# A two-layer graph network kernel: counting at 3.2 instead of 2.67 windows per lot, half of the one-hots on VectorE

## What is computed

```python
def reference(x, src, dst, edge_type_8, L0_gnn_weight, L0_gnn_bias, L1_gnn_W, L1_gnn_b):
    edge_index = jnp.stack([src, dst])
    h = jnp.maximum(_layernorm(x, axis=-1), 0.0)
    # layer 0: messages are h[src] @ weight[edge_type], summed at dst, plus bias
    x = x + _L0_gnn_ref(h, L0_gnn_weight, L0_gnn_bias, edge_index, edge_type_8)
    h = jnp.maximum(_layernorm(x, axis=-1), 0.0)
    # layer 1: dinv[dst] * dinv[src] * (h @ W)[src] summed at dst over the edges and a
    # loop at each node, plus b, then leaky_relu with slope 0.2
    x = x + _L1_gnn_ref(h, edge_index, L1_gnn_W, L1_gnn_b)
    return x
```

## Time and profile before

| | |
|---|---|
| median of three runs | 2302.07 us |
| lowest and highest | 2300.12 and 2308.04 us |
| the profiled execution's own time | 2306.06 us |
| its span in the profile | 2304.3 us |
| busy share of the span: PE, ACT, POOL, DVE | 87%, 70%, 71%, 53% |
| mean granted clock of PE | 0.953 |

### The profile page before, as it was taken

One profiled execution on the slowest core, in us unless ns is written; L12 is line 12 of the kernel. 1 busy time (PEld: TensorE's weight loads), 2 busy tenths in 40 slices (PEclk: granted clock), 3 DMA queues, 4 the chain that ended last, 5 costly groups with the idle time before them and its releaser, 6 DMA issues.

```text
span 2304.3 us, 44662 instructions
## 1 busy us (share of the span) xinstructions
PE 2007.3 (87%) x14354; PEld 1797.4 (78%) x14354; DVE 1219.7 (53%) x3510; ACT 1608.9 (70%) x3919; POOL 1643.0 (71%) x1740
## 2 busy tenths in 40 slices
PE   1567788887888898879899899999999999999897
PEld 1456777776787887768788889898888898989676
DVE  7446567667568666766656633323223232334267
ACT  4646677786878888678777877776767777676440
POOL 5577777777777777777766777777777777777414
PEclk9698999999999999999989999999999999999999
DMA  9446567656766776667776777765766666666485
GB/s 289 121 123 189 177 200 225 210 186 201 244 218 222 252 232 203 187 218 241 233 246 197 238 256 243 228 194 170 222 200 190 191 196 191 183 190 162 105 225 168
DMA packets 353088, 470.37 MB, mean 204 GB/s; under 512 B 113158, under 2 KB 264886, under 8 KB 352726
## 3 DMA queue, kind: packets, MB, share of 16 engines
q0 software_dynamic: 79072, 216.18, 31.9%
q1 hardware_dynamic: 228246, 165.07, 24.5%
q10 hardware_dynamic: 45536, 86.22, 10.2%
HBM read 348.61 MB, written 118.71 MB: 203 GB/s over the span
## 4 chain that ended last, share of the span: by engine, by line
PE 60%; POOL 13%; issue 7%; ACT 7%; DMA 5%; DVE 4%; ACTq 1%; DVEq 0%; POOLq 0%; SPq 0%
PE ps_slot L1599 21%; PE ps_slot L1659 13%; PE ps_proj L1615 13%; POOL rows_f L1099 12%; PE ps_aux L1659 9%; DMA rows_f<-table,idxT 3%; PE ps_slot L1629 3%; ACT gap_f L1338 2%; ACT staging_f L1275 2%; ACT wide_f L1331 1%; DMA abuf_f<-counts_d 1%; DVE hots_f L1495 1%; DVE hots_f L1492 1%; ACT onehot_f L1346 1%; ACT acc_f L1261 1%
## 5 line engine op out<-in xcount | busy, mean ns | idle before, releaser
L1099 POOL DMA_INDIRECT rows_f<-table,idxT x1617 | 1538.2, 951 | 510.3 <-issue 473.8
L1599 PE MATMUL ps_slot<-onehot_f,rows_f 128*128 128x128 f32 x6468 | 870.4, 287 | 150.7 <-DMA rows_f<-table,idxT 121.8
L1599 PEld LDWEIGHTS ps_slot<-onehot_f,rows_f 128*128 128x128 f32 x6468 | 824.8, 200 | 184.3 <-DMA rows_f<-table,idxT 134.7
L1338 ACT ACTIVATE gap_f<-iota,keyT 128x128 bf16<-128x128 bf16 x1617 | 528.6, 394 | 81.1 <-ACT staging_f L1275 49.6
L1275 ACT ACTIVATE staging_f<-ps_slot 128x400 bf16<-128x400 f32 x800 | 345.8, 500 | 182.2 <-PE ps_slot L1629 179.2
L1492 DVE TENSOR_TENSOR hots_f<-ps_slot,keys_f 128x400 bf16<-128x400 bf16 x800 | 285.2, 357 | 303.5 <-PE ps_slot L1629 299.5
L1615 PE MATMUL ps_proj<-w0t,acc_f 128*128 128x256 f32 x1600 | 375.8, 389 | 0.0
L1659 PE MATMUL ps_slot<-wide_f,stash_f 128*128 128x512 f32 (+1 forms) x1410 | 345.2, 390 | 1.6 <-ACT wide_f L1331 1.5
L1346 ACT ACTIVATE onehot_f<-gap_f 128x384 f32<-128x384 bf16 x539 | 277.5, 515 | 96.6 <-PE ps_slot L1599 96.4
L1416 DVE TENSOR_TENSOR acc_f<-ps_slot,acc_f 128x256 f32 x539 | 227.2, 422 | 219.5 <-PE ps_slot L1599 151.3
L1615 PEld LDWEIGHTS ps_proj<-w0t,acc_f 128*128 128x128 f32 x1600 | 303.2, 195 | 45.4 <-issue 1.6
(11 more groups left out here) (156 smaller groups left out, 871.5 us busy)
## 6 DMA issues: line engine op xcount, KB each, us to landing
abuf_f<-counts_d SPq DMA_DIRECT2D x66, 640.0 KB
rows_f<-table,idxT POOLq DMA_INDIRECT x1617
stash_f<-table SPq DMA_DIRECT2D x15, 1280.0 KB, 7.7
keys_f<-counts_d SPq DMA_DIRECT2D x30, 640.0 KB
table<-hs_f SPq DMA_DIRECT2D x50, 256.0 KB
table<-xres SPq DMA_DIRECT2D x10, 640.0 KB, 6.7
acc_f<-x_d SPq DMA_DIRECT2D x50, 128.0 KB, 2.7
x_d<-xt_f SPq DMA_DIRECT2D x49, 128.0 KB
```

The costliest lines, as they stand in the source:

```text
L1099: eng.indirect_dma_start(rows0[:, k, c, :], None, V["table0"], bass.IndirectOffsetOnAxis(ap=idxT[:, n * LOT + c:n * LOT + c + 1], axis=0)) ...
L1338: last = eng.activation(gap[:, n % 2, c, :], iota[:, :], ACT.Abs, scale=-1.0, bias=V["key"][:, n * LOT + c:n * LOT + c + 1])
L1599: last = eng.matmul(o[:, b * W:(b + 1) * W], rows0[:, k, c, b * P:(b + 1) * P], onehot[:, n % HOTS, c, :], start=(c == 0), stop=(c == LOT ...
```

## The change

- `last_window` goes from 3/8 to 5/16 of the number of windows (300 to 250 slots), so the rate of counting goes from 2.67 to 3.2 windows a lot, and windows now stand in pairs: a slot has 4 or 2 of them (4, 4, 2, 4, 2), where it had 3 or 2 (3, 3, 2).
- DVE builds the one-hots of a pair in one instruction of each kind (800 and 1024 elements a partition instead of twice 400 and twice 512), so it needs both buffers of the pair free. PE's count and ACT's evacuate are as they were, window by window, with three banks.
- For odd lots below `counts_end` (135 of them) DVE builds the lot's one-hot by one comparison of 384 elements with numbers in PSUM, in place of ACT's four activations. ACT builds the others, one step ahead as before. A new semaphore counts DVE's.
- The key steps move closer to a set's first window (look from 44 to 36 slots ahead, turn from 14 to 9, and so on).
- FIRST_BATCHES goes from 4 to 3, so the first phase has 18 units instead of 24.

The diff, cut to what matters:

```diff
-FIRST_BATCHES = 4
+FIRST_BATCHES = 3
+DVE_AHEAD = 3
@@ Plan
-        last_window = D.nsub * 3 // 8
+        last_window = D.nsub * 5 // 16
         self.win = {}
-        for w in range(D.nsub):
-            self.win.setdefault(FIRST_WIN + w * last_window // D.nsub, []).append(w)
+        for w in range(0, D.nsub, 2):
+            self.win.setdefault(FIRST_WIN + w * last_window // D.nsub, []).extend((w, w + 1))
-            self.turn_at[due - 14 if b else 10] = b
+            self.turn_at[due - 9 if b else 10] = b
@@ both_layers
+        lot_numbers = ps_slot[:, IOTA_BANK, (SPAN * P + MW) // 2:(SPAN * P + MW) // 2 + W]
+        odd_lots = [n for n in range(1, PL.counts_end, 2)]
+        other_lots = [n for n in range(PL.nlot) if n not in odd_lots]
+        turn_of_lot = {n: i for lots in (odd_lots, other_lots) for i, n in enumerate(lots)}
@@ scalar
+            def build_lot(n):
+                if n in other_lots:
+                    i = turn_of_lot[n] + 1
+                    if i < len(other_lots):
+                        build_gap(other_lots[i])
+                    build_onehot(n)
@@ vector
-                if w >= NHOT:
-                    eng.wait_ge(s_cnt, w - NHOT + 1)
+                if w >= NHOT:
+                    eng.wait_ge(s_cnt, w - NHOT + 2)
+                eng.tensor_tensor(hot_lo[:, a:a + 2, :, :], lo_numbers.unsqueeze(1).to_broadcast([P, 2, P, SPAN]),
+                                  lo_e[:, b % 2, k:k + 2, :].unsqueeze(2).to_broadcast([P, 2, P, SPAN]), ALU.is_equal).then_inc(s_hot, 1)
+            def build_onehot(n):
+                if n >= HOTS:
+                    eng.wait_ge(s_pe, n - HOTS + 1)
+                eng.tensor_tensor(onehot[:, n % HOTS, :, :], lot_numbers.unsqueeze(1).to_broadcast([P, LOT, W]),
+                                  V["key"][:, n * LOT:(n + 1) * LOT].unsqueeze(2).to_broadcast([P, LOT, W]), ALU.is_equal).then_inc(s_oh2, 1)
+                if n + DVE_AHEAD in odd_lots:
+                    build_onehot(n + DVE_AHEAD)
@@ tensor
-                eng.wait_ge(s_oh, n + 1)
+                eng.wait_ge(s_oh2 if n in odd_lots else s_oh, turn_of_lot[n] + 1)
-                eng.wait_ge(s_hot, w + 1)
+                eng.wait_ge(s_hot, w // 2 + 1)
+                eng.matmul(lot_numbers, identb[:, :], iota[:, :], start=True, stop=True)
```

More of the change, by code:

```diff
@@ L698, in __init__ @@
         self.tail = self.nlot + SEAM
-        last_window = D.nsub * 3 // 8
+        last_window = D.nsub * 5 // 16
         self.counts_end = FIRST_WIN + last_window + LEAD + 4
         self.win = {}
-        for w in range(D.nsub):
-            self.win.setdefault(FIRST_WIN + w * last_window // D.nsub, []).append(w)
+        assert D.nsub % 2 == 0 and NHOT % 2 == 0
+        for w in range(0, D.nsub, 2):
+            self.win.setdefault(FIRST_WIN + w * last_window // D.nsub, []).extend((w, w + 1))
         counted = [FIRST_WIN + (end * D.nw - 1) * last_window // D.nsub + LEAD + 9 for _, end in D.group]
@@ L708, in __init__ @@
             due = FIRST_WIN + b * P * last_window // D.nsub
-            self.look[due - 44 if b else 0] = b
+            self.look[due - 36 if b else 0] = b
             for i in range(len(PARTS)):
[L711 to L714, removed]
+                self.count_at[(due - 34 if b else 0) + i] = (b, i)
+            self.degree_out[due - 30 if b else 4] = b
+            self.degree_in[due - 28 if b else 6] = b
+            self.fetch[due - 22 if b else 5] = b
             for i in range(2):
-                self.key_at[(due - 18 if b else 8) + i] = (b, i)
-            self.turn_at[due - 14 if b else 10] = b
+                self.key_at[(due - 13 if b else 8) + i] = (b, i)
+            self.turn_at[due - 9 if b else 10] = b
         self.turn_win = {}
@@ L929, in both_layers @@
         s_oh = sem("onehot")
+        s_oh2 = sem("onehot_odd")
         s_deg = sem("degrees")
@@ L1280, in copy_keys @@
                 if b >= 2:
-                    eng.wait_ge(s_hot, P * (b - 1))
+                    eng.wait_ge(s_hot, P // 2 * (b - 1))
                 eng.wait_ge(s_tp, b + 1)
@@ L1333, in build_gap @@
             def build_gap(n):
-                if n >= 2:
-                    eng.wait_ge(s_oh, n - 1)
+                i = turn_of_lot[n]
+                if i >= 2:
+                    eng.wait_ge(s_oh, i - 1)
                 for c in range(LOT):
-                    last = eng.activation(gap[:, n % 2, c, :], iota[:, :], ACT.Abs, scale=-1.0, bias=V["key"][:, n * LOT + c:n * LOT + c + 1])
+                    last = eng.activation(gap[:, i % 2, c, :], iota[:, :], ACT.Abs, scale=-1.0, bias=V["key"][:, n * LOT + c:n * LOT + c + 1])
                 last.then_inc(s_gap, 1)
             def build_onehot(n):
-                eng.wait_ge(s_gap, n + 1)
+                i = turn_of_lot[n]
+                eng.wait_ge(s_gap, i + 1)
                 if n >= HOTS:
                     eng.wait_ge(s_pe, n - HOTS + 1)
-                eng.activation(onehot[:, n % HOTS, :, :], gap[:, n % 2, :, :], ACT.Relu, scale=-1.0, bias=1.0).then_inc(s_oh, 1)
+                eng.activation(onehot[:, n % HOTS, :, :], gap[:, i % 2, :, :], ACT.Relu, scale=-1.0, bias=1.0).then_inc(s_oh, 1)
             def copy_numbers():
@@ L1354, in _ @@
             build_gap(0)
+            def build_lot(n):
[4 more added lines that the diff above has]
+                    build_onehot(n)
             for n in range(AHEAD):
-                build_gap(n + 1)
-                build_onehot(n)
+                build_lot(n)
                 if n == 0:
@@ L1361, in _ @@
             for n in range(PL.slots):
[L1362 to L1365, removed]
+                build_lot(n + AHEAD)
                 if n - 1 in PL.turn_at:
@@ L1552, in _ @@
             eng.wait_ge(s_iota, 1)
+            eng.wait_ge(s_np, 1)
+            for n in range(DVE_AHEAD):
+                if n in odd_lots:
+                    build_onehot(n)
             off = None
@@ L1581, in _ @@
                     window_keys(*PL.key_at[n])
-                for w in PL.win.get(n, ()):
-                    build_hot(w)
+                for w in PL.win.get(n, ())[::2]:
+                    build_hots(w)
                 for k in PL.fin.get(n - 1, ()):
```

13 lines of the change are left out of this document (5 added, 8 removed).

## The result

The changed kernel takes 2415.94 us (median of four runs, 2411.68 to 2420.41) where the kernel before took 2301.1 in the same comparison: 1.0493 times as long, 95% interval 1.0476 to 1.051. That is 115 us slower. The forecast was 15 us slower, with 2338 us as its upper end.

The account below looks back on a forecast made before the run. POOL's gather pace is the floor; PE's 396 - 19 + 27 = 404 us against POOL's 360 leaves 44, less 18 absorbed, plus 6: 32 lost against 17, +15 us, 2317 us beside the median. Range, 8 in 10: 2288 to 2338.

Parts of the forecast that it names:

- The floor: Main part: POOL's own gather pace, 3.75 us a lot, which 539 lots cannot beat.
- the end: From the last gather to the end of the span: last units and projections, taken as unchanged at 138 us.
- The stretch: Slots 183 to 275, counting and dense product together, 93 lots: PE needs 404 us, POOL 360, a gap of 44.
- The ring's credit of 18 us: POOL's lead at slot 183, taken as 2.3 of up to seven lots, lets 18 us of the gap be absorbed.
- Step 3: Four windows in a slot with three banks: the fourth waits 0.55 us in 49 slots, 27 us.
- the old 24.8 us: PE's waits for ACT's evacuations and keys in the kernel before, 1023 to 1364 us, 82 lots.
- the 0.61 us: PE's waits and their consequences per lot in the kernel before, carried over to 93 lots as 57 us.
- Step 5: DVE builds windows in pairs, 1.10 us a pair instead of 1.20; taken at nothing, at most 6.3 us.
- Step 2: Half of the lots' one-hots leave ACT, so PE waits less for it: 19 us gained in 93 lots.
- Step 6: Key steps closer, shorter first phase, one matmul more, semaphore changes: taken at nothing.
- Steps 4 and 5: The first of these: a lot's one-hot on DVE takes about 0.56 us, adding 0.24 us a lot to DVE.
- The rival at 1.04 ns an element: DVE's pair comparison runs at one element a cycle, so DVE bounds 250 lots: 2490 us, chance 3%.
- The slower clock: Rival: the new waits slow PE's clock, 22 us on top, 2339 us, to 2370 with more; chance 7%.

Follow-up runs that it names:

- the first table: The changed kernel, seven edits of it, and two kernels that put half of the change into the kernel before; 2291.1 to 2457.4 us.
- LEAD 2: The changed kernel, but windows are counted two slots after DVE builds their one-hots, not three; 2355.2 us.
- act_onehots: The changed kernel, but ACT builds all lots' one-hots again; 2457.4 us.
- before_lead4: The kernel before, but windows are counted four slots after DVE builds them, not three; ratio 1.0165, repeated 1.0185.

## Why the prediction was wrong

The floor was right: 2282 to 2289 us plus what POOL loses, for the kernel before and the ten of the first table. So nearly was the end (142 us for 138). The prediction put POOL's loss at 32 us, and it was 126. The last counting matmul, told for near 1170 us, came at 1261 us. By its own steps:

- **The stretch was cut too short.** "The change part by part" sums slots 183 to 275 and takes the rest as free, because pieces pause in slots 160 to 182. 34.5 us were lost ahead of it. PE had slack there and waits ate it: in the kernel before PE's largest wait in 300:855 is for gathered rows, which is slack; in the changed kernel it is for evacuations. The two rows, before and after:

```profile
PE ps_slot L1599 <- DMA rows_f<-table,idxT: 38.8, 20, 5.7
...
PE ps_slot L1655 <- ACT staging_f L1283: 85.5, 74, 6.8
```

- **The ring's credit of 18 us was nearly all gone.** "I take POOL's lead at slot 183 as 2.3 lots" was 6.2 lots, which leaves 0.8 of a lot, 3 us. This follows from the step above.
- **Step 3 was sized by the shortest way.** 0.55 us for a fourth window took an ACT that is free and a wait that starts anew in each slot. In the stretch PE's 51 waits for an evacuation are 67.6 us, 1.3 us each. The sum had the old 24.8 us (28 us in 93 lots), 19 less for the relief and 27 more for the fourth windows, 36 us in all and with the waits for keys in it. The difference is 32 of the 45 us that PE took longer than forecast in the stretch:

```profile
PE ps_slot L1655 <- ACT staging_f L1283: 67.6, 51, 10.1
```

  "What a late ACT adds is in the 0.61 us" was the mistake in words. The 0.61 us were read from a kernel in which an evacuation was needed a slot later; now 150 windows need one of the same slot, so the same lateness of ACT costs more.
- **Step 5 put at nothing what turned out largest.** It says "DVE stands behind a later count than before" and takes that "at nothing, at most the 6.3 us of one old wait". LEAD 2 alone gave back 64 us, the most of any edit that keeps the rate; these 64 us are not a further term beside the others but lie in the longer waits and in the loss ahead of the stretch. The count of buffers was at hand: 8.0 windows ahead with eight buffers before, 9.6 after. A ring that was just full became a bound when the rate rose, and what stands behind the waiting instruction on DVE is what ACT, and through ACT PE, waits for: ACT's waits for the node tile's step were 6.8 us before, 37.2 after, 5.3 with LEAD 2.
- **Step 2, the relief of ACT, was right in kind**: 19 us forecast for the stretch, which has 46 or 47 of the 135 odd lots; 39 us measured for all of them (act_onehots, in part with a higher clock), 15 us in the kernel before, where only 18 were to be had. The stretch alone was not measured.
- **Step 6 in part.** The 43 pieces in the stretch were in the sum, but the shorter first phase, which put 13 of them there, was taken at nothing. Undoing it gave 38 us.
- **Steps 4 and 5, durations**: pairs took 569 and 679 ns (0.56 and 0.69 forecast), a lot's one-hot 547 ns (0.56). The rival at 1.04 ns an element is out. The slower clock was no large part of this loss: the granted clock of the stretch was 0.94 for 0.96, and the mean matmuls of its four groups took 1 to 2% longer (lots 287 ns for 283, halves 389 for 382), some 10 us of busy time.

The rows of the changed kernel for these durations:

```profile
L1508 DVE TENSOR_TENSOR hots_f<-ps_slot,keys_f 128x1024 bf16<-128x1024 bf16 x400 | 271.7, 679 | 0.0
L1505 DVE TENSOR_TENSOR hots_f<-ps_slot,keys_f 128x800 bf16<-128x800 bf16 x400 | 227.5, 569 | 304.1 <-PE ps_slot L1655 302.1 <-issue 1.5
L1515 DVE TENSOR_TENSOR onehot_f<-ps_slot,keyT 128x384 f32<-128x384 f32 x135 | 73.8, 547 | 1.4 <-PE ps_slot L1717 1.4
```

In the sum: the stretch took PE 449 us where 404 were forecast (45 more), the ring held 15 less, 34.5 were lost ahead, and 8 behind where 6 were forecast. 45 + 15 + 34.5 + 2 = 97, and 126 - 32 = 94 us of POOL's time is what was missed; the rest is rounding.

How the 42 us that stay with LEAD 2 and without rows of four divide between the first phase, the pairs and the fuller slots was not taken apart.

## What to carry to other kernels

When a rate goes up, work out for every ring how many items now lie between producer and consumer. Here a ring of buffers that was exactly as deep as that distance (8.0 windows, 8 buffers) turned its producer, at 9.6 windows, from an engine that keeps up into one that is dragged, and the price was paid by all that stands behind it in its program. A wait moved from the next slot into the same slot exposed the lateness of the engine waited for (1.3 us each), not the bare handshake (0.55 us). And where one engine has a fixed pace, count its lost time: it added up to the change in the span in all ten kernels of the first table, and told where to look. Count all of its releasers: in the other comparisons part of the lost time stood under a name other than PE.

## What the runs showed of the hardware

- One execution's span was the floor plus POOL's time lost to PE within 7 us in eleven kernels; there a gather that PE did not hold up followed the last one after 1.25 us.
- A comparison on DVE with one operand in PSUM and a 32-bit result, 384 elements a partition, takes 0.55 us, and took a lot's four activations (1.29 us on the chain) off ACT.
- In three comparisons the kernel before took 2744 to 2780 us instead of 2301 to 2306, over 17 to 19 runs each. In the traces from there DVE's one-hots and POOL's gathers are as long as elsewhere (in before_lead4 414 ns for 412, and 951 ns), the granted clock is 0.89 to 0.92, a lot's matmuls between 300 and 1000 us last 315 ns on average for 292, PE stands before matmuls without a named releaser, and POOL stands for 220 to 297 us before gathers with the releaser "remote". What that is stays open. The record numbers the chips of these comparisons 3, 4 and 7, and one numbered 4 also ran a comparison with the kernel before at 2306 us, so it can't be put down to the chip by what is known.
